# Relative terms of an attention block: low parts on other partitions, queries loaded a group ahead and copied on chip

## What is computed

```python
qkv = x @ qkv_w + qkv_b
qkv = qkv.reshape(B, S, 3, nh, hd).transpose(2, 0, 3, 1, 4)
qkv = qkv.reshape(3, B * nh, S, hd)
q, k, v = (qkv[0], qkv[1], qkv[2])
attn = jnp.einsum('bqd,bkd->bqk', q * scale, k)
Rh = _rel_gather(rel_pos_h, H)
Rw = _rel_gather(rel_pos_w, W)
qr = q.reshape(B * nh, H, W, hd)
rel_h = jnp.einsum('bhwc,hkc->bhwk', qr, Rh)
rel_w = jnp.einsum('bhwc,wkc->bhwk', qr, Rw)
bias = (rel_h[..., :, None] + rel_w[..., None, :]).reshape(B * nh, S, S)
attn = jax.nn.softmax(attn + bias, axis=-1)
```

## Time and profile before

| | |
|---|---|
| median of three runs | 2353.39 us |
| profiled execution, device time | 2349.04 us |
| its span in the trace | 2347.0 us |
| its mean granted TensorE clock | 0.923 |
| busy in the span: PE, DVE, ACT, POOL | 2053.8, 1452.2, 1501.9, 897.8 us |
| DMA queue of SP (q1): packets, MB, share of the 16 engines | 80640, 227.11, 42.2% |

### The profile page before, as it was taken

One profiled execution on the slowest core, in us unless ns is written; L12 is line 12 of the kernel. 1 busy time (PEld: TensorE's weight loads), 2 busy tenths in 40 slices (PEclk: granted clock), 3 DMA queues, 4 the chain that ended last, 5 costly groups with the idle time before them and its releaser, 6 DMA issues. The chain is left out here.

```text
span 2347.0 us, 34179 instructions
## 1 busy us (share of the span) xinstructions
PE 2053.8 (88%) x11132; PEld 1805.1 (77%) x11132; DVE 1452.2 (62%) x2321; ACT 1501.9 (64%) x2533; POOL 897.8 (38%) x609
## 2 busy tenths in 40 slices
PE   7933348999999999999999999975599999999998
PEld 6822227888888888888888888754488888989997
DVE  5654457999999999999999998455523624020000
ACT  3344406888888888888888888812155555555554
POOL 0020032333333333333333333472445656555553
PEclk9955568999999999999999999977599999999999
DMA  6778893465554555545556453253233524221111
GB/s 212 226 165 189 179 179 82 76 117 109 103 115 77 110 109 104 118 82 105 106 104 122 79 112 73 60 173 115 79 104 109 176 68 149 42 41 28 28 31 18
DMA packets 92437, 250.54 MB, mean 107 GB/s; under 512 B 9400, under 2 KB 43672, under 8 KB 86884
## 3 DMA queue, kind: packets, MB, share of 16 engines
q1 hardware_dynamic: 80640, 227.11, 42.2%
q0 software_dynamic: 10672, 20.46, 5.3%
q10 hardware_dynamic: 960, 0.80, 0.1%
HBM read 182.81 MB, written 65.52 MB: 106 GB/s over the span
## 5 line engine op out<-in xcount | busy, mean ns | idle before, releaser
L883 DVE TENSOR_REDUCE mx<-ps_m 128x1 f32<-128x384 f32 x1212 | 642.0, 552 | 100.8 <-PE ps_m L738 95.4
L595 POOL TENSOR_TENSOR p_lo<-p_f,p_hi 128x768 fp32r<-128x768 f32 x216 | 402.7, 1864 | 711.7 <-ACT p_f L842 711.7
L836 ACT ACTIVATE p_hi<-ps_s 128x768 fp32r<-128x768 f32 x648 | 528.7, 816 | 135.8 <-PE ps_s L752 132.3
L842 ACT ACTIVATE p_f<-ps_s 128x768 f32<-128x768 f32 x648 | 525.9, 812 | 12.6 <-POOL p_lo L595 12.5
L738 PE MATMUL ps_m<-key_hi,query_hi 128*128 128x384 f32 x1240 | 420.1, 345 | 51.7 <-DMA query_hi<-rel_hi_d 39.8
L595 DVE TENSOR_TENSOR p_lo<-p_f,p_hi 128x768 fp32r<-128x768 f32 x432 | 426.8, 988 | 36.5 <-ACT p_f L842 35.5
L749 PE MATMUL ps_s<-query_hi,key_hi 128*128 128x384 f32 x1296 | 338.0, 342 | 9.4 <-DMA query_rest<-m_d 7.4
L762 PE MATMUL ps_o<-p_hi,val 128*65 128x384 f32 x1296 | 331.6, 337 | 4.8 <-POOL p_lo L595 4.6
L752 PE MATMUL ps_s<-query_rest,key_rest 121*128 121x384 f32 x1296 | 331.9, 337 | 0.0
L762 PE MATMUL ps_o<-p_lo,val 128*65 128x384 f32 x1296 | 331.2, 337 | 0.0
L738 PEld LDWEIGHTS ps_m<-key_hi,query_hi 128*128 128x128 f32 x1240 | 232.5, 189 | 97.4 <-DMA query_hi<-rel_hi_d 40.1
(11 more groups left out here) (246 smaller groups left out, 2344.0 us busy)
## 6 DMA issues: line engine op xcount, KB each, us to landing
query_rest<-rel_lo_d SPq DMA_DIRECT2D x36, 864.0 KB
query_rest<-qk_lo_d SPq DMA_DIRECT2D x36, 576.0 KB
query_rest<-qk_hi_d SPq DMA_DIRECT2D x36, 576.0 KB
rel_lo_d<-out_lo SPq DMA_DIRECT2D x6, 1728.0 KB, 32.9
query_hi<-rel_hi_d SPq DMA_DIRECT2D x12, 864.0 KB, 17.2
w_raw__19777<-w_u SPq DMA_DIRECT2D x12, 768.0 KB, 5.8
w_raw__19778<-w_u SPq DMA_DIRECT2D x12, 768.0 KB, 4.3
w_raw__19779<-w_u SPq DMA_DIRECT2D x12, 768.0 KB, 4.5
```

The source lines that it names most:

```text
L595: engine.tensor_tensor(p_lo[r][:], p_f[idx % 2], p_hi[r][:].bitcast(F32), ALU.subtract).then_inc(lo_done(0, idx)[0], 1)
L836: act.activation(p_hi[r][:], ps_s[:, bank:bank + 2, 0:TB], ACT.Exp).then_inc(hi_ok, 1)
L842: act.activation(p_f[idx % 2], ps_s[:, bank:bank + 2, 0:TB], ACT.Exp).then_inc(f_ok, 1)
L883: dve.tensor_reduce(mx[s // TILES][:, s // 3 % 6, col:col + 1], ps_m[:, c, 0:TB], AX.X, ALU.max).then_inc(mx_ok, 1)
```

## The change

Each half's low part moves to partitions 64 to 111 of one tensor that holds both parts (`room` for a = 0, `out_both` for a = 1). `q_sb` is doubled, and groups 0 and 1 are both loaded at the start; group 2 is loaded after the two pairs of stores of group 0. A part is now two DMAs, high rows to partitions 0 to 31 and low rows to 32 to 63; GpSimd copies the high rows to 64 to 95 (`twice`), and the table's low part moves to rows 64 to 95 with them. PE waits for the load of a part and for its copy.

```diff
@@ -393,9 +393,11 @@
-        q_sb = sb("q_sb", [K3, HPT, S], F32R)
-        out_hi = [room[0:SIDE, :, :].bitcast(F32R), sb("out_hi", [SIDE, HPT, S], F32R)[:]]
-        out_lo = [sb(f"out_lo{a}", [SIDE, HPT, S], F32R)[:] for a in range(2)]
+        LOW_AT = 64
+        q_sb = [sb(f"q_sb{i}", [K3, HPT, S], F32R) for i in range(2)]
+        out_both = [room[0:LOW_AT + SIDE, :, :].bitcast(F32R), sb("out_both", [LOW_AT + SIDE, HPT, S], F32R)[:]]
+        out_hi = [o[0:SIDE] for o in out_both]
+        out_lo = [o[LOW_AT:LOW_AT + SIDE] for o in out_both]
...
@@ -416,29 +419,26 @@
             def load_q(g):
+                if g >= 2:
+                    sp.wait_ge(ps_ok, FILLS * (g - 1) + 1)
                 for part in range(Q_PARTS):
                     cols = slice(part * S // Q_PARTS, (part + 1) * S // Q_PARTS)
-                    for r, src in enumerate((qk_hi_d, qk_hi_d, qk_lo_d)):
-                        sp.dma_start(q_sb[r * HD:(r + 1) * HD, :, cols].bitcast(F32),
-                                     src[bass.ds(g * P, P), cols].rearrange("(h d) n -> d h n", d=HD)).then_inc(q_in[part], 16)
-
-            def group(g, last=False):
+                    for r, src in enumerate((qk_hi_d, qk_lo_d, qk_hi_d)[0:2]):
+                        sp.dma_start(q_sb[g % 2][r * HD:(r + 1) * HD, :, cols].bitcast(F32),
+                                     src[g * P:(g + 1) * P, cols].rearrange("(h d) n -> d h n", d=HD)).then_inc(q_in[g % 2][part], 16)
+
+            load_q(0)
+            load_q(1)
+            for g in range(GROUPS):
                 for n, a in enumerate(ORDER):
                     half = FILLS // 2
-                    if n == 1 and not last:
-
-                        sp.wait_ge(ps_ok, FILLS * (g + 1) + 1)
-                        load_q(g + 1)
...
-            load_q(0)
-            for g in range(0, GROUPS - 1):
-                group(g)
-            group(GROUPS - 1, last=True)
+                if g + 2 < GROUPS:
+                    load_q(g + 2)
@@ -449,9 +449,19 @@
-            pool.memset(neg_lo[HD:2 * HD, :], -1.0).then_inc(mask_ok, 1)
+            pool.memset(neg_lo[2 * HD:3 * HD, :], -1.0).then_inc(mask_ok, 1)
             pool.wait_ge(mask_ok, 2)
+            def twice(g):
+                for part in range(Q_PARTS):
+                    cols = slice(part * S // Q_PARTS, (part + 1) * S // Q_PARTS)
+                    pool.wait_ge(q_in[g % 2][part], 32 * (g // 2) + 32)
+                    pool.tensor_copy(q_sb[g % 2][2 * HD:3 * HD, :, cols], q_sb[g % 2][0:HD, :, cols].bitcast(F32)).then_inc(q_twice, 1)
+
+            twice(0)
+            twice(1)
+            pool.wait_ge(q_twice, 2 * Q_PARTS)
             one_hots(pool, key_hi, key_rest, hot[:], hot_ok)
+            twice(2)
@@ -461,13 +471,15 @@
-                        pe.wait_ge(q_in[f * CPB // (SIDE // Q_PARTS)], 48 * g + 48)
+                        part = f * CPB // (SIDE // Q_PARTS)
+                        pe.wait_ge(q_in[g % 2][part], 32 * (g // 2) + 32)
+                        pe.wait_ge(q_twice, Q_PARTS * g + part + 1)
```

More of the change, by code:

```diff
@@ L405, in phase_rel @@
         tab_ok = sem("tab_ok")
-        q_in = [sem(f"q_in{i}") for i in range(Q_PARTS)]
+        q_in = [[sem(f"q_in{n}_{i}") for i in range(Q_PARTS)] for n in range(2)]
+        q_twice = sem("q_twice")
         ps_ok = sem("ps_ok")
@@ L434, in group @@
                     for o, d in ((out_hi, rel_hi_d), (out_lo, rel_lo_d)):
-                        sp.dma_start(d[bass.ds(g * HPT, HPT), a * SIDE:(a + 1) * SIDE, :].rearrange("h r n -> r h n"),
+                        sp.dma_start(d[g * HPT:(g + 1) * HPT, a * SIDE:(a + 1) * SIDE, :].rearrange("h r n -> r h n"),
                                      o[a].bitcast(F32)).then_inc(r_out[a], 16)
-            load_q(0)
-            for g in range(0, GROUPS - 1):
-                group(g)
-            group(GROUPS - 1, last=True)
+                if g + 2 < GROUPS:
+                    load_q(g + 2)
             for a in range(2):
@@ L469, in _ @@
                         last = pe.matmul(ps[0:SIDE, bank, n * NQ:(n + 1) * NQ],
-                                         tab[:, a, SIDE - 1 - c:REL - c], q_sb[:, :, own], start=True, stop=True)
+                                         tab[:, a, SIDE - 1 - c:REL - c], q_sb[g % 2][:, :, own], start=True, stop=True)
                     last.then_inc(ps_ok, 1)
```

## The result

The changed kernel takes 2315.09 us (median, 2313.71 to 2318.48), the one before 2353.73 us beside it; the ratio is 0.9836, with a 95% interval of 0.9818 to 0.9854. It is faster by 38.6 us, where 25.4 us were forecast (2328.0). The profiled execution took 2313.71 us with a span of 2312.0.

A forecast was written before the change was run, and what follows sets the result against it. Bound: a chain between one DMA queue and the buffers it frees. Early loads, six store pairs and eight loads less overlap end the stage at 284.4 us, 25.4 us sooner: median 2353.39 becomes 2328.0 us, range 2298 to 2340.

The forecast's parts named there:

- What bounds the kernel: Stage of relative terms, 185.5 us: a chain between one DMA queue and the buffers it frees; DVE busy 86.59 us.
- rival 1: Stores on the two partition halves run side by side, 11.3 us a pair: 2282 us, or 2299 halfway; chance 0.21.
- my own case: A pair of stores takes 20.5 to 22.6 us, giving 2322 to 2340 us; chance 0.72.
- Loads: Query loads of three groups fall from 36 to 24: twelve at 1.353 us, 16.2 us less queue work.
- Order: Group 0's second store pair goes ahead of group 2's loads; group 1's compute needs no load standing behind stores.
- Copies: GpSimd's twelve casts of 32x2304 take 2.2 us each and cost nothing; at 3.9 us they cost 2 us.
- the clock's: TensorE's low clock reaches 63 us or more further into the next block's loop: over 0.2% slower; chance 0.03.
- the upper end of that case: Queue gains nothing but the loads, pair 22.6 us, overlap 2 us: 2337.5, or 2339.5 with copies at 3.9 us.
- Placement: Low parts on partitions 64 to 111: a pair of stores takes 21.5 us, near the serial 22.6 us.
- The sum: Landing of the stage's last store pair: 149.6 + 6 x 21.5 + 8 x 1.353 - 5 = 284.4 us.
- 4 us to spare: Group 2's last computed half is ready 4 us before the store pair ahead lands, so the queue stays fed.
- SP was held: Loads issued while stores are queued hold SP; if worse, stage ends near 307 us, within 0.2%; chance 0.04.

The follow-up runs named there:

- the second profile of the same kernel: The changed kernel run once more, unaltered, beside the by-heads kernels: 2316.02 us, ratio 0.9834.
- the second set of transfers: Changed kernel with more transfers alone behind the stage, finer cuts, 32-partition stores and query loads: sets took 9.8, 12.4, 20.4, 53.3, 13.9 and 12.5 us.

## Why the prediction was right, and where it was off

**What bounds the kernel** held: a queue and the buffers that it frees, with DVE, the busiest engine, at work for 85.56 of 148.6 us. All that was gained lies between 124 and 310 us. The forecast of 2328.0 was 12.9 us too high: 11.3 us in the stage, 3.0 since the profiled execution stood 1.4 us below the median and not 4.35, less some 1.4 in the rest. That the time lies in the range is owed to its lower part, which I had taken over from rival 1; my own case, with its chance of 0.72, did not come.

**Loads**: 24 are left and the twelve are worth 6.5 us of the stage. Their price was mis-sized: 1.353 us came from parts with a third load to partitions 64 to 95. With both on one half it is (151.55 - 130.99) / 14 = 1.47 us; eight loads alone show the same difference (13.9 us to one half, 12.5 in turn). The sixteenth had landed by 151.55, not 149.6.

**Order**: right, 6.7 us when taken back alone. **Copies**: 2.10 us where 2.2 was taken, hidden as said; the first half of group 0 was stored at 146.39 for 146 forecast. The last copy of group 1 ends at 153.65 and the one-hots behind it cost nothing. Group 2's copies start at 193.10 and PE needs them after 212. Two figures beside the forecast do not come out of their own terms: a half that ends at 150.5 is 0.9 us behind 149.6 and not 2, and the clock's (25.4 + 4.7) / 0.5 is 60 us and not 63. Neither entered the 2328.0; the first makes the upper end of that case, 2339.5, 1 us too high.

**Placement**: this step failed, as a term of the sum that was mis-sized. I took 21.5 us a pair "near the serial end"; in a chain it is 18.2 (72.9 / 4), against 23.3 on one half, both with the set's one issue and landing spread over four pairs. I had read from 216 GB/s of loads, a third of them to the other half, that halves do not add up. That row is of 32-partition DMAs; alone two of those do take the sum of their times (12.5 us), and in turn eight loads gain only a tenth. In stores of 48 partitions the way of 0 to 15 carries twice the bytes (0 to 47 take 12.7 us, 0 to 31 take 7.1), and a lone pair ends at half its rate. I read from this that some DMA engines are done early, step into the next DMA, and find the other half free; that placement on both halves is the cause is shown, but no view here tells the DMA engines apart, so this step is argued. I had named it in the forecast and given it 1 us a pair; it is 5. The Trainium skill's 6% for two DMAs on two halves (SBUF — State Buffer, "Can I just issue two DMAs to hit both halves?") is near what the lone pair gains (4%, 23.2 against 24.2) and the two whole DMAs of 32 partitions (nothing), but fits neither the chain (22% less) nor the cut by heads (35% less than 24.2).

**The sum** with 18.2 us a pair is 151.55 + 5 x 18.2 + 10.8 - 5 = 248.4 for the fifth pair. It landed at 251.0, so in the kernel a pair comes out at (251.0 - 151.55 - 10.8 + 5) / 5 = 18.7 us if the other two terms are right. The last pair was not ready behind it in time. Of the "4 us to spare" 1.5 were left with quicker pairs: ACT began that half when the fourth pair had landed, 231.75, DVE ended at 249.48, and the last pair was issued at 249.56. But from 244 on the queue had carried only 38 GB/s, so this pair ran alone and took 23.5 us, 22.1 of them behind the fifth. So five pairs, 2.8 us quicker each, gave 13.9 us; the early loads took 2.0 back and the last pair 0.6 (22.1 for 21.5). That is 11.3 us, from the forecast 284.4 to 273.07.

**Rivals**: a part of rival 1, the halves beside each other, is what came; its 11.3 us a pair did not. SP was held (4.13 us for a load) and reached group 1's stores at 188.49, as worked out (189), 1.5 us before the second pair had landed. The queue was no longer full then (share 0.69 at 184 to 188); what that costs was tried only by heads, where loads behind the stores gave nothing. The clock: 0.50 through the stage as before, and the remainder of the program 1.7 us longer; in the second profile of the same kernel that remainder is 2049.8 us for 2038.9, so 1.7 us is within what two executions differ by.

## What to carry over

A DMA queue whose rate and share fall while its last transfers run (here from 207 to 106 GB/s and from 0.96 to 0.60) has room left; give it something that goes another way, and set that next to them in the queue, in small pieces. Before a rate is taken for a bound of another shape, ask whether the two shapes load the same paths equally. And where transfers get quicker, look which wait was about to become the last: here it was the half that ACT and DVE make behind the fourth pair, with 4 us to spare on paper and 1.5 in the trace.

## What the runs showed that I had not expected

- Half the bytes from 0 to 15 take as long as all from 0 to 31: 7.07 against 7.12 us. The forecast had no term for it; ahead of that run it was one of two outcomes.
- One pair of stores can take 24.2, 23.2, 20.4, 15.8 or 15.2 us for the same bytes, by placement and by how finely the halves alternate (whole, two heads, one head, two queues).
- Two queues do what the cut by heads does: 15.2 us, with two instructions (554.36 to 569.58, and again 394.85 to 410.06 in the second set of transfers). It was measured alone, not in the kernel, where ACT or GpSimd would have to wait for DVE to issue them.
